# Routed experts of a two-layer gated block: rows of the ninth expert and later gathered by GpSimd instead of loaded by SyncE

## The reference

```
scores = softmax(flat @ Wr + router_bias)            # 2048 tokens, 64 experts
topk_scores, topk_idx = top_k(scores, 4)             # then normed to sum 1
pos = place of the token in its expert's queue       # valid if pos < CAP = 128
xb[eid, pos] = flat[tok]                             # empty slots are zero
h = silu(xb @ Wg) * (xb @ Wu);  yb = h @ Wd          # for each of the 64 experts
out[tok] += yb[eid, pos] * w * valid                 # four experts for a token
out += shared experts of flat
```

## Time and profile before

| | us |
|---|---|
| median of 3 runs (lowest to highest) | 1108.14 (1107.43 to 1109.08) |
| profiled execution, its own time | 1115.18 |
| its span, first to last instruction | 1113.5 |
| TensorE busy in the span | 1024.4 |
| VectorE, ScalarE, GpSimd busy | 722.2, 500.2, 584.8 |
| mean DMA rate over the span | 179 GB/s |

### The profile page before, as it was taken

One profiled execution on the slowest core, in us unless ns is written; L12 is line 12 of the kernel. 1 busy time (PEld: TensorE's weight loads), 2 busy tenths in 40 slices (PEclk: granted clock), 3 DMA queues, 4 the chain that ended last, 5 costly groups with the idle time before them and its releaser, 6 DMA issues. The chain is left out here.

```text
span 1113.5 us, 18851 instructions
## 1 busy us (share of the span) xinstructions
PE 1024.4 (92%) x5364; PEld 738.3 (66%) x5364; DVE 722.2 (65%) x1704; ACT 500.2 (45%) x880; POOL 584.8 (53%) x555
## 2 busy tenths in 40 slices
PE   4999999999879999998899999999999999999960
PEld 2555555565437777775389468577778888888850
DVE  3678778777448888886688248167306666667650
ACT  3666656655238888886432211311304333333320
POOL 6566676674326667665524646356432344333551
PEclk9999999999889999999899999999999999999985
DMA  8467655577645332331540241043269999999729
GB/s 268 151 220 249 205 166 179 192 248 283 240 160 167 104 109 104 103 113 67 185 142 18 91 137 48 11 138 112 87 208 333 337 331 308 288 316 336 190 29 194
DMA packets 128254, 199.49 MB, mean 179 GB/s; under 512 B 35975, under 2 KB 44167, under 8 KB 128186
## 3 DMA queue, kind: packets, MB, share of 16 engines
q1 hardware_dynamic: 106394, 160.40, 42.6%
q0 software_dynamic: 21360, 37.48, 13.1%
q10 hardware_dynamic: 432, 0.79, 0.2%
HBM read 133.10 MB, written 87.56 MB: 198 GB/s over the span
## 5 line engine op out<-in xcount | busy, mean ns | idle before, releaser
L957 POOL TENSOR_TENSOR m_down_lo<-wo,m_down_hi 128x512 fp32r<-128x512 f32 x78 | 129.8, 1684 | 76.3 <-ACT m_down_hi L1053 76.3
L566 PE MATMUL bank<-win,vT 128*128 128x512 f32 x256 | 126.6, 609 | 0.0
L734 DVE TENSOR_REDUCE negmax<-bank 128x1 bf16<-128x512 f32 x128 | 85.6, 672 | 43.3 <-PE bank L573 42.9
L659 ACT ACTIVATE win<-bank 128x512 f32<-128x512 f32 x128 | 69.5, 595 | 92.3 <-PE bank L558 89.9
L1067 DVE TENSOR_TENSOR m_up_lo<-w,m_up_hi 128x1024 fp32r<-128x1024 f32 x78 | 95.5, 1226 | 12.4 <-ACT m_up_hi L1025 11.5
L2075 POOL DMA_INDIRECT out<-m_y,m_token x32 | 51.2, 1600 | 87.1 <-DMA out<-m_y,m_token 47.1
L1304 POOL DMA_INDIRECT tab<-stage_up,slot x64 | 65.6, 1025 | 53.3 <-DVE slot L1650 35.4
L2105 PE MATMUL bank<-y,m_w 128*128 128x128 f32 x736 | 89.7, 275 | 0.0
L2219 ACT ACTIVATE sh_gate_a<-bank 128x512 f32<-128x512 f32 (+1 forms) x40 | 20.5, 512 | 151.4 <-PE bank L2212 121.9
L2075 POOL DMA_INDIRECT sums<-m_y,m_token x32 | 50.6, 1581 | 71.7 <-DVE m_y L2169 41.9
L2105 PEld LDWEIGHTS bank<-y,m_w 128*128 128x128 f32 x736 | 86.4, 193 | 0.1
(11 more groups left out here) (302 smaller groups left out, 2492.8 us busy)
## 6 DMA issues: line engine op xcount, KB each, us to landing
tab<-zeros SPq DMA_DIRECT2D x16, 1056.0 KB
m_w<-in_L_ffn_Wg SPq DMA_DIRECT2D x46, 256.0 KB
m_w<-in_L_ffn_Wu SPq DMA_DIRECT2D x46, 256.0 KB
m_w<-in_L_ffn_Wd SPq DMA_DIRECT2D x46, 256.0 KB
m_x<-tab SPq DMA_DIRECT2D x39, 256.0 KB, 2.7
ytab<-m_y SPq DMA_DIRECT2D x39, 256.0 KB, 2.0
stage_up<-tab SPq DMA_DIRECT2D x32, 264.0 KB
m_x<-tab SPq DMA_DIRECT2D x32, 264.0 KB
```

Of the source, the lines that this page charges most:

```text
L566: nc.tensor.matmul(pO[s * 2 + h][:], vT[:, s, sb_, h:h + 2, :].rearrange("p a c -> p (a c)"), probs[:, sb_ % 2, h, :], start=(sb_ == 0), s ...
L659: nc.scalar.activation(probs[:, b % 2, h, :], pS[h][:], ACT.Exp, scale=1.0 / HEAD).then_inc(p_ready, 1)
L734: nc.vector.tensor_reduce(negmax[:, s, m:m + 1], rough_bank(k, m)[:], AX.X, ALU.max, negate=True).then_inc(pm_read, 1)
L957: nc.gpsimd.tensor_tensor(dn_lo[:, m, :], row(wo0, e * MB + m), dn_hi[:, m, :], ALU.subtract).then_inc(dn_lo_ready, 1)
```

## The change

The rows of experts 0 to 7 are loaded by SyncE as before, all eight ahead of the loop. For experts 8 to 63 SyncE's load goes, and GpSimd gathers the rows: when it comes to expert e it first waits for y of e, then issues the gather for expert e + 7 (`X_AHEAD`), and only then waits for the earlier scatter and scatters e. The gather's index is the row in `tab1`, plus 1048576 where the slot is empty, which is out of bounds, so an empty slot keeps what was in the slot before. The counts come from one matmul of ones with the running counts `chosen1` before the loop, and two VectorE operations make `empty` (0 or `NO_TOKEN` for each slot and expert) and the indices. As an empty slot no longer holds an invalid token number, VectorE takes the maximum of the row's number and `empty`; for that the token number is now stored as a float. TensorE waits for weights and gathered rows on two semaphores. The four semaphores of the gathers of `middle` are used again for them.

```diff
+X_AHEAD = 7
+        def weights_of(e):
+            n = e % W_RING
+            return loaded[n], 48 * (e // W_RING + 1) + (16 if n < X_RING else 0)
         @block.sync
-            for e in range(X_EARLY, X_RING - 1):
+            for e in range(X_EARLY, X_RING):
                 load_rows(sp, T, e)
...
-                e = i + X_RING - 1
-                if e < E1:
-                    need(sp, xT_full, i)
-                    need(sp, y_ready, max(i - 1, min(i, 1)))
-                    load_rows(sp, T, e)
         @block.gpsimd
             for e in range(E1):
+                pool.wait_ge(y_ready, e + 1)
+                n = e + X_AHEAD
+                if X_RING <= n < E1:
+                    pool.wait_ge(back_read, 1)
+                    pool.wait_ge(rows_in[n % TPB], 32 * B + 16 * ((n - X_RING) // TPB))
+                    nc.gpsimd.indirect_dma_start(
+                        row_slot(T, n % X_RING), None, T["tab1"], bass.IndirectOffsetOnAxis(row_at[:, n:n + 1], 0),
+                        bounds_check=E1 * CAP1 - 1, oob_is_err=False).then_inc(rows_in[n % TPB], 16)
                 if e == JOIN:
...
                 if e >= SUMS:
                     pool.wait_ge(added[e % SUMS], entries(e))
-                pool.wait_ge(y_ready, e + 1)
                 nc.gpsimd.indirect_dma_start(
         @block.tensor
+            nc.tensor.matmul(pB[1][:, 0:E1], T["onesb"][:], T["chosen1"][:], start=True, stop=True).then_inc(back_full, 1)
...
-                    pe.wait_ge(loaded[e % W_RING], 64 * (e // W_RING + 1))
+                    pe.wait_ge(*weights_of(e))
+                    if e >= X_RING:
+                        pe.wait_ge(rows_in[e % TPB], 32 * B + 16 * ((e - X_RING) // TPB + 1))
         @block.vector
+            dve.wait_ge(back_full, 1)
+            nc.vector.tensor_scalar(empty[:], pB[1][:, 0:E1], T["rowid"][:, 0:1], float(NO_TOKEN), ALU.is_le, ALU.mult)
+            dve.drain()
+            nc.vector.scalar_tensor_tensor(row_at, T["base1"][:], T["rowid"][:, 0:1], empty[:], ALU.add,
+                                           ALU.add).then_inc(back_read, 1)
...
-                    nc.vector.tensor_copy(token[:, m:m + 1], r[:, 0:1].bitcast(I32))
+                    nc.vector.tensor_tensor(token[:, m:m + 1], r[:, 0:1], empty[:, i:i + 1], ALU.max)
```

More of the change, by code:

```diff
@@ L157, in build @@
                 T["hidden"] = T["stage_gate"][:].rearrange("p s (n t) -> p (s n) t", t=SEQ)
+                T["gathered"] = [staged.enter_context(nc.semaphore(f"rows_gathered_{j}")) for j in range(TPB)]
                 T["s_w1"] = [staged.enter_context(nc.semaphore(f"m1_loaded_{n}")) for n in range(W_RING)]
@@ L379, in _ @@
             pool.drain()
-            nc.gpsimd.iota(zeros[:, D:D + 1].bitcast(I32), [[0, 1]], base=NO_TOKEN, channel_multiplier=1)
+            nc.gpsimd.iota(zeros[:, D:D + 1], [[0, 1]], base=NO_TOKEN, channel_multiplier=1,
+                           allow_small_or_imprecise_dtypes=True)
             nc.gpsimd.memset(vT[:, :, :, 1, :], 1.0)
@@ L1195, in middle @@
             "mid_small_loaded", "shared_gate_loaded", "shared_back_loaded"))
-        gathered = [sem(f"y0_gathered_{j}") for j in range(TPB)]
+        gathered = T["gathered"]
         beta_ready, wexp_ready = sem("beta_ready"), sem("wexp_ready")
@@ L1640, in place @@
                 nc.vector.tensor_reduce(wsum[:], wt1[:], AX.X, ALU.add)
-                nc.vector.tensor_copy(flat[:, :, D:D + 1].bitcast(I32), tokens[:, g * TPB:g * TPB + TPB].unsqueeze(2))
+                nc.vector.tensor_copy(flat[:, :, D:D + 1], tokens[:, g * TPB:g * TPB + TPB].unsqueeze(2))
                 nc.vector.tensor_copy(flat[:, :, D + 1:D + 1 + TOP1], idxf[:])
@@ L2005, in experts @@
         match = sb("m1_match", [P, TOP1])
+        empty, row_at = T["chosen1"], T["base1"][:].bitcast(I32)
+        rows_in = T["gathered"]
         xT = T["y0"][:, TPB - 1].rearrange("p k (b t) -> p k b t", b=DB)
@@ L2065, in _ @@
             for e in range(E1):
+                pool.wait_ge(y_ready, e + 1)
[6 more added lines that the diff above has]
+                        bounds_check=E1 * CAP1 - 1, oob_is_err=False).then_inc(rows_in[n % TPB], 16)
                 if e == JOIN:
-                    pool.wait_ge(back_read, LATE)
+                    pool.wait_ge(back_read, LATE + 1)
                     pool.wait_ge(added[e % SUMS], entries(e) - 16)
@@ L2082, in _ @@
                 nc.gpsimd.dma_start(whole[n], part[n], max_dma_last_dim=2 * 4 * D, accum_op=ALU.add).then_inc(joined, 16)
-            pool.wait_ge(back_read, LATE + TPB + 1)
+            pool.wait_ge(back_read, LATE + TPB + 2)
             nc.gpsimd.dma_start(T["out_rows"].rearrange("(t p) d -> p t d", p=P)[:, TILES - TPB:, :], rest[:],
@@ L2110, in _ @@
                         if n == 0:
-                            need(pe, back_read, j - 1)
+                            need(pe, back_read, j)
                         tile = (AT_ONCE + j) % TPB
@@ L2137, in _ @@
                     nc.scalar.activation(g[:, s, :], pH[s][:, 0:CAP1], ACT.Silu).then_inc(g_ready, 1)
-                    act.wait_ge(loaded[i % W_RING], 64 * (i // W_RING + 1))
+                    act.wait_ge(*weights_of(i))
                     need(act, y_full, i - 1)
@@ L2172, in _ @@
                     j = back_at(i - 1)[0]
-                    dve.wait_ge(back_full, j + 1)
+                    dve.wait_ge(back_full, j + 2)
                     if j == 0:
```

## The result

The changed kernel takes 1114.71 us (median of 11 runs, 1111.87 to 1117.91) against 1108.91 us (11 runs, 1106.56 to 1109.72) of the kernel before on the same chip: 5.8 us slower. The forecast was 1114.5. The profiled execution took 1117.91 us, its span is 1116.2.

The account below looks back on a forecast made before the run. The prediction took TensorE, busy 92% of the span, as the bound. Stall +4.3, clock +2.3, head +0.1 and tail -0.3 made +6.4 us, so 1108.14 became 1114.5 us, range 1107.7 to 1121.

Parts of the forecast that it names:

- The sum, +6.4: Whole kernel: stall +4.3, clock +2.3, head +0.1 and tail -0.3 us, all reaching the end.
- TensorE waits once, at expert 41: Loop, transposes of expert 41: its gather, issued at expert 34 behind the accumulate, stalls TensorE 4.3 us (0 to 8.4).
- The rival in which less traffic brings the accumulate home early: At JOIN: accumulate lands by 980.5, gather 41 takes some 5 us, stall under 1.5 us, near 1108.5; chance 0.19.
- The price by the Trainium skill: Gather of expert 41: about 2 us plus bytes at 436 GB/s, 2.6 us when full; stall 1.9 us.
- The place in the ring: At JOIN: gather 41 stands behind the 87 rows of scatter 33, taken as 6 us to landing.
- The clock: TensorE after the stall at expert 41: half clock costs 2.3 us, 0 after a stall under 2 us.
- The head, 0.1: Before the loop: one added 64-column matmul on TensorE costs 0.1 us; the two vector operations are hidden.
- One more semaphore wait 56 times, 0: Before the transposes on TensorE's queue: an added wait costs 0, between 0 and 0.05 us each.
- GpSimd's cycle has room: Loop on GpSimd: gather 1.25 us plus scatter 1.98 us is 3.2 of 3.82 us per expert, if waits are already satisfied.
- The rival of a cycle without room: Loop on GpSimd: cycle 3.9 against 3.82 us, lag grows, TensorE loses +14 us, with JOIN stall about 1125; chance 0.10.
- Dropped slots are worth nothing in the loop: Loop: queues lose about 56% of row bytes, but TensorE never waited for rows or weights; gain 0.
- The tail, -0.3: After the last y: scatter of expert 63 waits less for that of expert 61, saving 0.3 us (0 to 4.3).

## Why the prediction was right, step by step

**The sum, +6.4: right in size, and its last digits are luck.** The medians differ by 5.8 us, and the ratio's interval is 5.2 to 7.5 us of 1108.91. The two large terms, forecast at 4.3 and 2.3, are 4.5 and 2.8 in one profile, 4.0 and 1.3 in the other, so the sum itself moves by 2 us from execution to execution. The profiled execution was forecast at 1121.6 and took 1117.91: its loop is longer by more than the sum, but it began 6.75 us earlier (830.85 instead of 837.60), which the change has no part in.

**TensorE waits once, at expert 41, for the gather issued behind scatter 33: right, and shown.** Moving the distance (6, 8) or JOIN moves the wait to experts 40 and 49 or ends it, and without the accumulate it is gone. The size was 4.3 by forecast and 4.5 and 4.0 in two profiles. The steps under it: 1.06 us for a gather on GpSimd (0.95 forecast) with the gap of 0.30 as forecast; 10.27 us of wait for the accumulate (10.09 in the earlier trace rows); from gather 41 to the transposes 5.9 and 5.5 us (6 forecast). From issue to landing the 56 gathers took 2.4, 5.4 and 7.3 us (least, median, most), near the gathers of the earlier trace rows. The rival in which less traffic brings the accumulate home early did not come about: it took as long as before, with the DMA engines at 1.06 of their time in the window before it landed, as in the earlier trace rows.

**The price by the Trainium skill: too low here.** The estimate by the Trainium skill ("DMA: Bandwidth & Descriptors", Anatomy of one DMA) was 2.6 us for a full gather. The prediction makes 989.1 and a wait of 1.9 us of it; from its own start of gather 41, 985.5, it comes to 988.1 and 0.9. The wait was 4.5 and 4.0, so the rows decide. The empty gather of expert 49 shows that the extra is not in its bytes.

**The place in the ring: not shown to matter.** The prediction put gather 41 behind scatter 33, on the order in a ring that the Trainium skill states ("DMA: Bandwidth & Descriptors", Queues, rings and completion order). The runs show no price for it: 5.1 and 5.6 us ahead of the scatter against 5.9, 5.5 and 4.6 behind one. The 6 us came out, but the reason given for them is not shown. The weights on the other queue fit a little better. Full gathers at this place took 3.7 and 4.6 us (gathers behind the waits, and six ahead) where queue q1 took 36 and 34% of the DMA engines' time meanwhile, and 5.1 to 5.9 us in the changed kernel and with the gather ahead of the scatter, where it took 60 to 73%. But with all slots gathered it was 5.9 us at 42%, and no run changes that load by itself, so what makes the 6 us stays open.

**The clock: right in kind, 2.3 us forecast, 2.8 and 1.3 measured.** It varies: after a wait of 4.51 us two windows are at half clock, after 3.99 one. It doesn't grow with the wait either: behind waits of 6.3, 6.9 and 8.0 us (all slots, six ahead, gathers behind) the iteration lost 1.4, 1.8 and 2.0 us, because the half clock begins inside a long wait. My bound that nothing is lost after a wait under 2 us held once (1.71) and failed once (1.94). Keeping TensorE busy through the wait kept the clock.

**The head, 0.1: no cost found.** The matmul starts 0.03 us before the first transposes (830.82 and 830.85 in TensorE's timeline) and is run into them. Moving it changes nothing that can be measured. The half clock behind it occurs before the change too, in one profile of two.

**One more semaphore wait 56 times, 0: right.** Outside of the one stall the iterations keep 3.82 us, and with eight ahead the ratio is 1.0000.

**GpSimd's cycle has room: right.** GpSimd is busy 649.5 us instead of 584.8, and its queue doesn't fall behind. The forecast sign, a smaller lag behind y after expert 45, came, but mostly for another reason. The y of expert 47 and its scatter after the change, from the timelines of VectorE and GpSimd:

```profile
1025.01 0.75 DVE L2189 TENSOR_SCALAR m_y<-bank,m_weight 128x512 f32<-128x512 f32 x1
...
1031.22 1.66 POOL L2087 DMA_INDIRECT out<-m_y,m_token  x1 [0.76 <-DMA out<-m_y,m_token]
```

That is 6.2 us. Before it was 13.3 (1022.64 to 1035.98), and 15.8 in the second profile. But TensorE, and so y, is held up by 4.5 and 2.8 us at expert 41, and that alone is 7.3. With eight ahead, where it isn't held up, the lag at expert 47 is 11.0 us:

```profile
1025.42 0.75 DVE L2189 TENSOR_SCALAR m_y<-bank,m_weight 128x512 f32<-128x512 f32 x1
...
1036.41 1.59 POOL L2087 DMA_INDIRECT out<-m_y,m_token  x1 [0.30 <-issue]
```

So GpSimd does catch up with the gathers added to its queue, and this lag, below the two of before, is what shows that it has room. The rival of a cycle without room falls at this distance, but the gathers placed behind the waits show it near: eight waits and 1.0167.

**Dropped slots are worth nothing in the loop: right, as far as the runs can tell.** The rows' bytes fell (46.10 MB of all in 870 to 1050), and the two large queues' share went from 0.99 to 0.90. TensorE had waited for no transfer, so it gained nothing. Moving all slots costs nothing that the ratio shows, though the wait in its one profile is 1.8 us longer.

**The tail, -0.3: not found.** The wait between the last y and the last scatter fell from 4.3 us to 3.6 (1080.56 to 1084.18), but the tails as a whole are 35.6 and 34.1 us after, 35.4 and 34.8 before, more apart within a kernel than between the two.

## What to carry to other kernels

When a load moves onto a queue that also waits for landings, look for the longest wait on that queue and ask which load is the first behind it: the distance ahead must cover that wait, here 10.3 us and a scatter, and not the usual cycle. Issuing ahead of an expert's own waits isn't enough, since each one is still behind those of the expert before, and one more expert of distance took all of the loss away. A short stall of TensorE is to be priced with the half clock behind it, here 1.3 to 2.8 us for stalls of 1.9 to 8.0 us and not in proportion to them (one of 1.7 cost none), and bytes saved off the critical path should be priced at nothing.

## What the runs showed of the hardware

- A gather with no valid row (expert 49) is waited for until 4.7 us after its start, with a full scatter ahead of it and the DMA engines at 1.04.
- Dropped slots of the gathers leave some small packets: 8294 under 512 B from 870 to 1050, against 6663 where the gathers move all slots and 6768 before the change.
- The length of a wait alone doesn't decide the half clock. The same wait of 1.8 us before the loop was followed by it in 11 of the 14 profiles, but not in the first of the kernel before, nor with all slots gathered, nor with the gathers behind the waits. Behind JOIN 1.71 us left the clock at 1.00, 1.94 gave 3.4 us at 0.51, 3.99 gave 3.4 us and 4.51 and 4.56 gave 6.8 us.
- The half clock can begin inside a wait: at 6.87 us it began 3.4 us before the wait ended.
- One matmul of 128 columns in float32 leaves two records, and 24 of them took 5.35 us, 0.22 us each; the four transposes of a 128x512 tile leave four records and take 0.47.
